# Expert quarters between histogram chunks, and openings that wait only for what they use

## The chip, the cores and the metric

The program runs on one core of a Trainium2 chip. The metric is the device time of one execution in microseconds (us); the times shown are the median and the spread of three runs.

## The reference, cut to what matters

The input is x, 8 images of 32 x 32 tokens with 256 channels (8192 tokens). Four stages follow one another, each with a residual:

```python
x = x + retention(_ln_c(x))            # 8 heads of 32, decayed scores, group norm, gelu, Wo
t = t + moe(_ln_t(t), edges0)          # expert layer 0
x = x + int8_conv_3x3(_ln_c(x))
t = t + moe(_ln_t(t), edges1)          # expert layer 1

def moe(x, ...):
    h = (x @ W_gat).reshape(M, HEADS, NUM_EXPERTS)       # graph attention over 1048576 edges
    e = leaky_relu(a_src[src] + a_dst[dst])
    alpha = exp(e - e_max[dst]) / denom[dst]
    agg = segment_sum(h[src] * alpha, dst) + b_gat
    scores = layernorm(agg).mean over heads              # -> top 2 of 4 experts, softmax
    for ei in range(4):
        hh = gelu(x @ W1[ei] + b1[ei])                   # 256 -> 512
        out += gate[ei] * (hh @ W2[ei] + b2[ei])         # 512 -> 256
```

Edges name nodes up to 65536, and out-of-range indices are clamped for reading and dropped for adding. So an edge counts where its target is one of the 8192 tokens: most of those have the last token as their source and only need to be counted per target (a histogram), and the rest are listed one by one. The experts' products need no edge, so TensorE can do them in any gap before the gates are known.

## The kernel before, in words

The program is written in raw engine queues: each engine (SP, POOL, ACT, DVE, PE) has one instruction stream and waits on semaphores; the order of the work is the order in the source. The functions are `attention_layer`, `ffn_layer` (twice) and `conv_layer`, with a barrier of all engines between them.

**Attention.** `turn(-1)` is the opening: it loads the first image, makes its statistics (DVE `statistics`, `variances`), the power on POOL (L279), the normalised image on ACT (`normal`, L337), its transposes and first projections on PE (L604, L542). The eight images follow in turns 0 to 7. Ahead of `turn(-1)`, DVE centres the value weights (L475 to L480) and waits for the rotation tables (`s_rot_t`), ACT and PE wait for the small constants (`s_small`: `blk`, `sel`, `gb`), which SP loads last of all, behind 7.5 MB of decay tables (L220 to L225).

**Expert layer.** Tokens stand in 16 blocks of 512. 64 pairs (block, expert) are to be computed; the first 40 (`PRE_PAIRS`) are done while the graph part runs, 16 in the window loop, the last 8 with the gates known. A pair is 16 quarters: `fourths(n, ...)` on PE (L1144) issues n quarters, of which two of four are one up-product each (`up`, L1128) and two are two down-products each (`down`, L1139); `experts(n)` and `pre(n)` are 4n quarters. The 40 pairs are 656 quarters. ACT follows with the gelu (`gelu`, L1333), eviction and bias, in the same order of pairs.

The stages of a layer, in order, with what PE gets between its own work (all by `pre`):
1. Opening: SP loads the first block of x, its edges, 15 constants, then block 1 (L933 to L956). DVE, ACT and PE wait for all 15 (`s_const`, L1166, L1376, L1499).
2. Nodes, 16 blocks: DVE moments, edge scan, normalising; PE transposes and `heads`; quarters by `PRE_NODES`.
3. Lists: DVE takes the largest 8 of each segment, three times; 33 x 4 quarters (`PRE_LISTS`).
4. Halves: 52 half-steps that rank and place list entries; PE gets 2 quarters in each.
5. Unit: one more list unit (`unit_products` L1250 on PE, `unit_places` on DVE, four half-steps that pass results back and forth). PE does `pre(PRE_UNIT)` = 24 quarters before it. DVE then sorts (`sort`), makes the targets and releases POOL (`turn_to_next`).
6. Rounds: four times, DVE takes eight keys of each of 32 segments (`eights_of_key`), their digits, and 8 pairs of one-hot matrices (`hots`, L1525); PE multiplies each pair into the histogram (`chunk`, L1199). DVE may be two pairs ahead. PE does `pre(PRE_ROUND)` = 52 quarters before the 8 chunks.
7. Late chunks and the open loop: one more pass of keys, two smaller chunks, then a loop of `n_round` passes, which runs twice here. PE does `pre(PRE_LATE)` = 72 quarters ahead of the late chunks.
8. Window: counts, the last 24 quarters, another unit, then the segmented scans on DVE, for which POOL has gathered rows since stage 5 (64 scatters L1066, 168 gathers L1073). PE runs the 16 looped pairs; ACT stops inside them for two exponentials, the first after `IN_SCAN` = 6 steps (`s_xm`).
9. Gates and tail.

## Time and profile before

| | |
|---|---|
| median of three runs | 4097.9 us (4090.67 to 4099.19) |
| profiled execution, its own time | 4094.64 us |
| its span | 4092.9 us, 49913 instructions |
| PE busy, DVE busy | 86%, 71% of the span |
| mean granted TensorE clock | 0.935 |
| attention / expert layer 0 / conv / expert layer 1 | begin at about 0, 1250, 2546 and 2792 us |

A row of the timeline gives its start in us from the beginning of the span, its length, the engine, the line of the kernel, what is written and read, and how many instructions are merged in it; the bracket is the time the engine stood idle before, and what ended that. A product in float32 appears as two records, so 4 records of L1128 are two up-products, and 8 of L1139 four down-products.

### The profile page before, as it was taken

The page shows a single profiled execution, that of the slowest core. Times are in us where ns is not written, and L with a number is a line of the kernel's source. Part 1 is how long each engine was busy: PE and PEld are TensorE (multiplying, and loading weights), DVE is VectorE, ACT ScalarE, POOL GpSimd, SP SyncE. Part 2 cuts the span into 40 slices and gives each one's busy share as a digit, 9 for nine tenths or more (in the row PEclk, how much of TensorE's full clock was granted, in tenths as well). Part 3 has the DMA queues.
Part 4 walks back from the last instruction along what each step waited for, and adds up shares of the span by engine and source line. Part 5 has one row for each costly group of instructions (what it writes and reads, how often), then busy time and mean ns, then how long its engine had stood idle before and what let it go on. Part 6 is the DMA issues. An engine that isn't in the chain of part 4 may idle for free. (4 is left out here: it accounts for less than half of the span.)

```text
span 4092.9 us, 49913 instructions
## 1 busy us (share of the span) xinstructions
PE 3513.5 (86%) x16818; PEld 2016.4 (49%) x16818; DVE 2885.9 (71%) x6290; ACT 1489.9 (36%) x2073; POOL 1616.9 (40%) x1146
## 2 busy tenths in 40 slices
PE   4999999999985999969878987585999969878987
PEld 2233333333324765646555654464665646555655
DVE  2676676676666798797779336876788797778337
ACT  2565565555552632212223321231632212223321
POOL 2776676666770000058863401000000048872500
PEclk9999999999995999989989998786999989989999
DMA  3000000010005410001121347215410001122337
GB/s 145 11 22 11 32 32 13 20 32 22 11 21 200 163 53 27 32 22 41 32 62 56 138 147 280 78 64 199 174 48 32 32 22 36 37 42 70 138 133 273
DMA packets 151250, 307.24 MB, mean 75 GB/s; under 512 B 24932, under 2 KB 107492, under 8 KB 145892
## 3 DMA queue, kind: packets, MB, share of 16 engines
q1 hardware_dynamic: 100516, 186.28, 12.7%
q10 hardware_dynamic: 25920, 94.38, 6.0%
q0 software_dynamic: 24576, 23.41, 3.3%
q8 instruction: 149, 2.44, 0.3%
q14 instruction: 89, 0.73, 0.1%
HBM read 186.18 MB, written 117.83 MB: 74 GB/s over the span
## 5 line engine op out<-in xcount | busy, mean ns | idle before, releaser
L1128 PE MATMUL l_pu<-l_tt,l_w 128*128 128x512 f32 x2048 | 1005.3, 612 | 52.7 <-ACT l_hid L1333 38.9
L1139 PE MATMUL l_pd<-l_w,l_hid 128*128 128x256 f32 x4096 | 985.2, 383 | 12.2 <-ACT l_hid L1333 12.2
L1139 PEld LDWEIGHTS l_pd<-l_w,l_hid 128*128 128x128 f32 x4096 | 782.2, 193 | 310.9 <-issue 226.7
L1333 ACT ACTIVATE l_hid<-l_pu,l_b 128x512 f32<-128x512 f32 x512 | 349.9, 687 | 1177.7 <-PE l_pu L1128 1170.1
L389 DVE TENSOR_TENSOR at_pr<-at_ps,at_decay 128x1024 f32<-128x1024 f32 x512 | 600.7, 1215 | 179.7 <-PE at_ps L503 178.7
L307 ACT ACTIVATE at_ab<-at_pr 128x1024 f32<-128x1024 f32 x512 | 537.1, 1055 | 435.6 <-DVE at_pr L389 392.1
L258 POOL TENSOR_TENSOR at_ab<-at_ab 128x1024 f32<-128x1024 f32 x256 | 601.2, 2372 | 176.8 <-ACT at_ab L307 176.8
L1128 PEld LDWEIGHTS l_pu<-l_tt,l_w 128*128 128x128 f32 x2048 | 388.4, 196 | 322.7 <-issue 300.4
L1073 POOL DMA_INDIRECT l_g<-hs_rows,l_i_src x336 | 409.6, 1219 | 102.5 <-issue 102.5
L1066 POOL DMA_INDIRECT spots<-l_ad,l_i_row x128 | 160.4, 1253 | 608.2 <-DVEq L1731 569.8
L503 PE MATMUL at_ps<-at_qr,at_kr 32*128 32x512 f32 x2048 | 348.9, 643 | 13.9 <-issue 8.9
L1199 PE MATMUL l_ph<-l_one_lo,l_one_hi 128*128 128x256 bf16 x1104 | 137.3, 281 | 172.1 <-DVE l_one_hi L1525 172.1
L522 PE MATMUL at_ps_av<-at_pr,at_v 128*32 128x512 f32 x2048 | 277.0, 608 | 6.9 <-ACT at_o L315 5.1
L1525 DVE TENSOR_TENSOR l_one_lo<-l_iota,l_lo 128x4096 bf16<-128x4096 bf16 (+1 forms) x72 | 158.1, 2196 | 123.8 <-PE l_ph L1199 123.1
L542 PE MATMUL at_ps<-at_xnT,at_wt 128*128 128x512 f32 x512 | 239.0, 610 | 6.8 <-DVE at_t L410 4.1
L1347 ACT ACTIVATE l_yst<-l_pd 128x512 f32<-128x512 f32 x224 | 133.8, 597 | 249.9 <-PE l_pd L1139 249.9
L503 PEld LDWEIGHTS at_ps<-at_qr,at_kr 32*128 32x128 f32 x2048 | 106.7, 184 | 234.0 <-issue 168.0
L1358 ACT ACTIVATE l_pd<-l_b 128x512 f32<-128x512 f32 x256 | 153.9, 601 | 168.9 <-DVEq L1967 114.6
L1199 PEld LDWEIGHTS l_ph<-l_one_lo,l_one_hi 128*128 128x128 bf16 x1104 | 106.3, 100 | 202.6 <-DVE l_one_hi L1525 187.9
L1954 DVE SCALAR_TENSOR_TENSOR l_xo<-l_yb,l_gates,l_xo 128x256 f32<-128x256 f32 x448 | 187.3, 480 | 15.5 <-DMA l_yb<-ys 7.9
L1082 POOL DMA_INDIRECT l_res<-found,l_i_row x128 | 122.7, 958 | 180.1 <-DMA found<-l_rows 141.7
L542 PEld LDWEIGHTS at_ps<-at_xnT,at_wt 128*128 128x128 f32 x512 | 92.9, 191 | 153.7 <-issue 125.6
(362 smaller groups left out, 4169.2 us busy)
## 6 DMA issues: line engine op xcount, KB each, us to landing
ys<-l_yst ACTq DMA_DIRECT2D x112, 512.0 KB, 2.7
l_yb<-ys SPq DMA_DIRECT2D x28, 2048.0 KB, 10.1
l_tt<-tT ACTq DMA_DIRECT2D x36, 512.0 KB, 3.4
at_xt<-in_x SPq DMA_DIRECT2D x16, 1024.0 KB, 5.3
l_xt<-x SPq DMA_DIRECT2D x32, 512.0 KB, 4.1
tT<-l_xnT ACTq DMA_DIRECT2D x32, 512.0 KB, 4.6
l_xo<-x SPq DMA_DIRECT2D x28, 512.0 KB, 4.9
x<-at_xt SPq DMA_DIRECT2D x8, 1024.0 KB, 4.3
```

What stands on the lines that cost most here:

```text
L258: pool.tensor_tensor(size(2 * k, p), size(2 * k, p), size(2 * k + 1, p), ALU.add).then_inc(s_sum, 1)
L307: act.activation(size(n // 2, n % 2), pr[:, n % 4, :, :], ACT.Abs).then_inc(s_a, 1)
L389: dve.tensor_tensor(pr[:, n % 4, :, :], ps[slot("s", n)][:, :, :], decay[:, h:h + 2, first:first + HALF], ALU.mult).then_inc(s_ring[slot(" ...
L503: ins = pe.matmul(ps[slot("s", n)][:, jj, :], kr[rows, hq, P * kb:P * kb + P], qr[rows, hq, HALF * qn:HALF * qn + HALF], start=True, stop= ...
L522: ins = pe.matmul(ps_av[KD * j:KD * j + KD, :], v[:, kb, KD * h:KD * h + KD], pr[:, (2 * u + j // 2) % 4, j % 2, :], start=(kb == 0), stop ...
L542: ins = pe.matmul(ps[slot(what, i)][:, s, :], wt[:, 2 * (i // 2) + s, k, P * hq:P * hq + P], xnT[:, k, HALF * (i % 2):HALF * (i % 2) + HAL ...
L1073: pool.indirect_dma_start(g[:, j, :], None, hs_rows[:, :], bass.IndirectOffsetOnAxis(ap=i_src[:, j:j + 1].bitcast(U32), axis=0)).then_inc( ...
L1128: ins = pe.matmul(ps_u[q % 2][:, :], w1[:, e, c, P * q:P * q + P], tt[:, s, c, :], start=(c == 0), stop=(c == KK - 1))
L1139: ins = pe.matmul(ps_d[r // 2][:, C * (r % 2):C * (r % 2) + C], hid[:, k % 2, c, P * r:P * r + P], w2[:, k % GE, c, :], start=False, stop= ...
L1199: ins = pe.matmul(hist, one_hi[:, q % 2, j:j + 2, :].rearrange("p a b -> p (a b)"), one_lo[:, q % 2, j:j + 2, :].rearrange("p a b -> p (a ...
L1333: act.activation(hid[:, k % 2, q, :], ps_u[q % 2][:, :], ACT.Gelu, bias=b1[:, k % GE, q:q + 1]).then_inc(s_act, 1)
L1954: ins = dve.scalar_tensor_tensor(xo[:, b, r, :], yb[:, b, MTT * q + r, :], gates[:, MTT * t + r, q:q + 1], xo[:, b, r, :], ALU.mult, ALU.add)
```

## The change

- Attention: the ten small loads go from SP, behind the decay tables, to POOL's queue, ahead of its `turn(-1)`. ACT and PE wait for them after `turn(-1)`. DVE centres the values after the statistics (at u = 18), and PE waits for `s_cen` at the projections.
- Expert layer, opening: `ident` has its own semaphore and is loaded after block 0; block 1 goes ahead of the other constants; `w_gat`, `att_src`, `att_dst` and `iota` are loaded by ACT's queue. DVE does moments and normalising of block 0, then the score columns, then the scan. All other constants are waited for at block 2 (ACT) or after the nodes (DVE, PE).
- Quarters on PE (ACT's order of work is the same, its split into calls is dropped): the stage of lists and halves is unchanged.

| quarters | before | after |
|---|---|---|
| ahead of the unit | 24 | 0 |
| after the unit | 0 | 52 |
| each round, ahead of its chunks | 52 | 32 |
| each round, after each of 8 chunks | 0 | 2 |
| ahead of the late chunks | 72 | 40 |
| ahead of the open loop | 0 | 20 |
| left for the window | 24 | 24 |

```diff
-ROUNDS1 = 0
-PRE_ROUND = 13
+PRE_ROUND = 8
+PRE_CHUNK = 2
-PRE_LATE = 18
-PRE_UNIT = 6
+PRE_LATE = 10
+PRE_OPEN = 5
+PRE_UNIT = 13
...
@@ attention, SP and POOL
-            sp.dma_start(blk[:, :], blk_in).then_inc(s_small, 16)
-            sp.dma_start(sel[:, :], sel_in).then_inc(s_small, 16)
-            for j in range(HPQ):
-                sp.dma_start(gb[KD * j:KD * j + KD, 0:1], ln_g).then_inc(s_small, 16)
-                sp.dma_start(gb[KD * j:KD * j + KD, 1:2], ln_b).then_inc(s_small, 16)
...
             pool.memset(nhalf[:, :], -0.5).then_inc(s_cst, 1)
+            pool.dma_start(blk[:, :], blk_in).then_inc(s_small, 16)
+            pool.dma_start(sel[:, :], sel_in).then_inc(s_small, 16)
+            for j in range(HPQ):
+                pool.dma_start(gb[KD * j:KD * j + KD, 0:1], ln_g).then_inc(s_small, 16)
+                pool.dma_start(gb[KD * j:KD * j + KD, 1:2], ln_b).then_inc(s_small, 16)
@@ attention, ACT and PE
-            act.wait_ge(s_small, 16 * (2 + 2 * HPQ))
             turn(-1)
+            act.wait_ge(s_small, 16 * (2 + 2 * HPQ))
...
-            pe.wait_ge(s_cen, 1)
-            pe.wait_ge(s_small, 16 * (2 + 2 * HPQ))
             turn(-1)
+            pe.wait_ge(s_small, 16 * (2 + 2 * HPQ))
@@ experts, PE
             def histogram(s_at):
                 for q in range(RC // HIST):
                     chunk(q, HIST, s_at(q))
+                    pre_part(PRE_CHUNK)
...
-            pre(PRE_UNIT)
             unit_products(xu, n_u)
+            pre(PRE_UNIT)
-            for r in range(ROUNDS1, ROUNDS0):
+            for r in range(ROUNDS0):
                 pre(PRE_ROUND)
                 histogram(lambda q: r * (RC // HIST) + q + 1)
             pre(PRE_LATE)
             for k, width in enumerate(LATE_CHUNKS):
                 chunk(CHUNKS0 + k, width, CHUNKS0 + k + 1)
+            pre(PRE_OPEN)
             pe.wait_ge(s_round, 1)
@@ experts, DVE
-            dve.wait_ge(s_mem, 1)
-            dve.wait_ge(s_const, CONSTS)
...
-            for b in range(NBLK):
+            moments(0)
+            normal(0)
+            score_columns()
+            scan(0)
+            for b in range(1, NBLK):
                 moments(b)
                 scan(b)
                 normal(b)
-                if b >= 1:
-                    drain(b - 1)
+                drain(b - 1)
             drain(NBLK - 1)
+            dve.wait_ge(s_mem, 1)
+            dve.wait_ge(s_const, CONSTS)
@@ experts, ACT
-            act.wait_ge(s_const, CONSTS)
-            act.wait_ge(s_open, 2)
+            act.dma_start(wg[:, :, 0:GF], w["w_gat"]).then_inc(s_gat_in, 16)
+            act.dma_start(a_s[:, :], w["att_src"].to_broadcast([P, GF])).then_inc(s_gat_in, 16)
+            act.dma_start(a_d[:, :], w["att_dst"].to_broadcast([P, GF])).then_inc(s_gat_in, 16)
+            act.dma_start(iota[:, :], consts["iota_row"]).then_inc(s_gat_in, 16)
```

How the instructions of an engine stand in the program (no times in these rows; the lines of the changed kernel are shifted by 5 to 7 in this part):

PE at the end of the halves and the unit, before (`l_pr` are the banks of ranks and of the table, L1276 reads the count of units):

```order
L1232 MATMUL l_pr<-l_sent,l_one 128x336 x3
L1270 MATMUL l_ph<-l_zero 128x256
L1276 TENSOR_LOAD l_n_unit
L1276 ISA x2
L1128 MATMUL l_pu<-l_tt,l_w 128x512 x2
L1139 MATMUL l_pd<-l_w,l_hid 128x256 x4
```

and of the change:

```order
L1239 MATMUL l_pr<-l_sent,l_one 128x336 x3
L1277 MATMUL l_ph<-l_zero 128x256
L1280 TENSOR_LOAD l_n_unit
L1280 ISA x2
L1259 UNCONDITIONAL_BRANCH
L1259 ISA
L1225 MATMUL l_pr<-l_one,l_above 128x384
L1227 MATMUL l_pr<-l_one,l_ones 128x256
```

The unit's first product now follows the load of the count; the 24 quarters that stood between are gone from here.

PE in a round, before: the 8 chunks of 16 products in one piece, with quarters on both sides (`l_ph` is the histogram bank):

```order
L1128 MATMUL l_pu<-l_tt,l_w 128x512 x2
L1139 MATMUL l_pd<-l_w,l_hid 128x256 x4
L1199 MATMUL l_ph<-l_one_lo,l_one_hi 128x256 x128
L1128 MATMUL l_pu<-l_tt,l_w 128x512 x2
L1139 MATMUL l_pd<-l_w,l_hid 128x256 x4
```

and of the change:

```order
L1144 MATMUL l_pd<-l_w,l_hid 128x256 x4
L1204 MATMUL l_ph<-l_one_lo,l_one_hi 128x256 x16
L1133 MATMUL l_pu<-l_tt,l_w 128x512 x2
L1204 MATMUL l_ph<-l_one_lo,l_one_hi 128x256 x16
L1144 MATMUL l_pd<-l_w,l_hid 128x256 x4
L1204 MATMUL l_ph<-l_one_lo,l_one_hi 128x256 x16
```

Each chunk is now followed by two quarters, in turn two up-products and four down-products.

ACT in the attention's opening, before, with what it waits for:

```order
L337 ACT_TABLE_LOAD [waits at_rstd]
L337 ACTIVATE at_xn<-at_xt,at_shift,at_rstd 128x256 [waits at_small]
```

and of the change:

```order
L337 ACT_TABLE_LOAD
L337 ACTIVATE at_xn<-at_xt,at_shift,at_rstd 128x256 [waits at_rstd]
```

The table load waits for nothing any more, and the small constants are waited for at the first magnitude of turn 0.

## Rows read from the trace of the kernel before

**Rows 1.** The page's part 1: engines' busy time, share, instructions.

```profile
PE 3513.5 (86%) x16818; PEld 2016.4 (49%) x16818; DVE 2885.9 (71%) x6290; ACT 1489.9 (36%) x2073; POOL 1616.9 (40%) x1146
```

**Rows 2.** Timeline of layer 0, PE, expert quarters: start, us, engine, line, out<-in, count.

```profile
1840.79 1.89 PE L1139 MATMUL l_pd<-l_w,l_hid 128*128 128x256 f32 x8
1842.51 1.88 PE L1128 MATMUL l_pu<-l_tt,l_w 128*128 128x512 f32 x4
```

**Rows 3.** Timeline, PE, histogram chunks of layer 0; in brackets idle time before.

```profile
1806.62 6.49 PE L1199 MATMUL l_ph<-l_one_lo,l_one_hi 128*128 128x256 bf16 x32 [29.19 <-DVE l_one_hi L1525]
...
1876.95 3.66 PE L1199 MATMUL l_ph<-l_one_lo,l_one_hi 128*128 128x256 bf16 x32
...
1945.58 3.66 PE L1199 MATMUL l_ph<-l_one_lo,l_one_hi 128*128 128x256 bf16 x32
```

**Rows 4.** Timeline, DVE, the round between: eight largest per segment, then the one-hot pairs.

```profile
1830.29 10.54 DVE L1535 MAX8 l_cand<-l_key 128x8 f32<-128x256 f32 x32
...
1855.38 2.29 DVE L1525 TENSOR_TENSOR l_one_lo<-l_iota,l_lo 128x4096 bf16<-128x4096 bf16 x1
...
1858.73 2.29 DVE L1525 TENSOR_TENSOR l_one_lo<-l_iota,l_lo 128x4096 bf16<-128x4096 bf16 x1
```

**Rows 5.** Timeline, DVE, the unit of layer 0.

```profile
1721.74 0.29 DVE L1640 SCALAR_TENSOR_TENSOR l_sent<-l_pr,l_one 128x128 f32<-128x128 f32 x1 [18.33 <-PE l_pr L1220]
```

**Rows 6.** Timeline, DVE and PE, late chunks and open loop: layer 0, then layer 1.

```profile
2036.92 10.55 DVE L1535 MAX8 l_late<-l_key 128x8 f32<-128x256 f32 x32
...
2067.31 2.29 DVE L1525 TENSOR_TENSOR l_one_lo<-l_iota,l_lo 128x4096 bf16<-128x4096 bf16 x1
...
2102.90 1.23 DVE L1525 TENSOR_TENSOR l_one_lo<-l_iota,l_lo 128x2048 bf16<-128x2048 bf16 x1 [11.21 <-PE l_ph L1199]
...
3668.02 1.89 PE L1199 MATMUL l_ph<-l_one_lo,l_one_hi 128*128 128x256 bf16 x8 [20.12 <-DVE l_one_hi L1525]
...
3671.54 3.73 PE L1128 MATMUL l_pu<-l_tt,l_w 128*128 128x512 f32 x4
```

**Rows 7.** Instructions of one line, POOL's indirect DMAs of layer 0, with times to landing.

```profile
L1066 POOL DMA_INDIRECT spots<-l_ad,l_i_row x64: 955/962/3037, 1778.8 to 1877.4; - x64
...
L1073 POOL DMA_INDIRECT l_g<-hs_rows,l_i_src x168: 942/947/3037, 1878.6 to 2133.4; - x168
...
DMA to landing us min/median/max: 2.3/2.7/4.6
```

**Rows 8.** Timeline, DVE, first use of the gathered rows, layer 0.

```profile
2172.46 1.54 DVE L1823 TENSOR_TENSOR l_e<-l_g,l_adj 128x672 f32<-128x672 f32 x1 [0.55 <-DVE l_adj L1818]
```

**Rows 9.** Timeline, ACT of layer 1, after the gathered rows are used.

```profile
3722.03 1.28 ACT L1414 ACT_TABLE_LOAD   x1 [1.22 <-DVE l_xm L1830]
```

**Rows 10.** Timeline, the attention's opening; then DMAs to landing, POOL's own issues.

```profile
18.30 2.71 DVE L431 BATCH_NORM_STATS2 at_stats<-at_xt 128x6 f32<-128x256 f32 x8 [6.12 <-DMA at_sin<-in_sin]
...
22.24 1.67 POOL L279 TENSOR_TENSOR at_rstd<-at_ve,at_nhalf 128x8 f32<-128x8 f32 x1 [21.34 <-DVE at_ve L443]
...
38.13 4.04 ACT L337 ACTIVATE at_xn<-at_xt,at_shift,at_rstd 128x256 f32<-128x256 f32 x8 [12.57 <-DMA at_gb<-in_ln_b]
...
at_decay<-in_decay SPq DMA_DIRECT2D x2, 3840.0 KB, 27.3
at_xt<-in_x SPq DMA_DIRECT2D x2, 1024.0 KB, 5.4
...
L1045 POOL DMA_DIRECT2D hs_rows<-l_hs x32: 750/752/963, 1282.9 to 2972.6; - x32
```

**Rows 11.** Timeline, DVE and SP, opening of expert layer 0; x to landing.

```profile
1249.99 0.37 SPq L933 DMA_DIRECT2D l_xt<-x  x1
...
1263.88 0.29 DVE L1500 CAST l_pc<-l_iota 128x128 f32<-128x128 bf16 x1 [19.51 <-DMA l_b<-in_L_b]
...
1273.71 1.39 DVE L1455 BATCH_NORM_STATS2 l_stats<-l_xt 128x6 f32<-128x256 f32 x4
...
l_xt<-x SPq DMA_DIRECT2D x10, 512.0 KB, 4.3
```

More of the change, by code:

```diff
@@ L449, in invert, with centre_values @@
                     dve.reciprocal(sd[:, cols], sd[:, cols]).then_inc(s_rsd, 1)
+                def centre_values():
+                    dve.wait_ge(s_wt, 16)
+                    wv = wt[:, 4, :, :].rearrange("p k (h d) -> p (k h) d", d=KD)
+                    dve.tensor_reduce(vsum[:, :], wv, AX.X, ALU.add).then_inc(s_csum, 1)
+                    dve.wait_ge(s_csum, 1)
+                    dve.scalar_tensor_tensor(wv, vsum[:, :].unsqueeze(2).to_broadcast([P, KK * H, KD]), -1.0 / KD, wv,
+                                             ALU.mult, ALU.add).then_inc(s_cen, 1)
+                    dve.wait_ge(s_rot_t, 64)
                 for u in range(NQ):
+                    if b == -1 and u == 18:
+                        centre_values()
                     if tail and u == SPREAD + 1:
@@ L538, in project @@
                 def project(what, hq, i):
+                    if b == -1:
+                        pe.wait_ge(s_cen, 1)
                     pe.wait_ge(s_ring[slot(what, i)], free(what, i))
@@ L940, in _ @@
             block_edges(0)
-            for into, from_ in ((ident, consts["ident"]), (first, consts["first"]), (above, consts["above"]), (not_above, consts["not_above"]), (places, consts["places"]), (iota, consts["iota_row"]),
+            sp.dma_start(ident[:, :], consts["ident"]).then_inc(s_ident, 16)
+            block_x(1)
+            block_edges(1)
+            for into, from_ in ((first, consts["first"]), (above, consts["above"]), (not_above, consts["not_above"]), (places, consts["places"]),
                             (part, consts["part"])):
                 sp.dma_start(into[:, :], from_).then_inc(s_const, 16)
-            sp.dma_start(wg[:, :, 0:GF], w["w_gat"]).then_inc(s_const, 16)
-            sp.dma_start(a_s[:, :], w["att_src"].to_broadcast([P, GF])).then_inc(s_const, 16)
-            sp.dma_start(a_d[:, :], w["att_dst"].to_broadcast([P, GF])).then_inc(s_const, 16)
             for k, v_ in enumerate((w["b_gat"], w["ln_gamma"], w["ln_beta"])):
@@ L1731, in turn_to_next @@
                 dve.sem_inc(s_first, 1)
-            rounds(0, ROUNDS1)
-            restart()
             unit_places(xu, n_u)
```

46 lines of the change are left out of this document (18 added, 28 removed).

## The prediction

> **What bounds the kernel now.** I read the page first. PE is busy for 86% of the span [rows 1], so an average says PE; but the product work is a fixed stock, and what matters is where PE waits and where it makes DVE wait. So I went through the timeline of PE and DVE, stage by stage, then asked on which engine each wait ends.
>
> A unit of four quarters is 1.72 us of down-products and 1.72 us of up-products, one starting at 1840.79 and the next at 1842.51 [rows 2]: a quarter is 0.86 us. 656 quarters of a layer are 564 us of PE.
>
> A round lasts 68.6 us, from 1876.95 to 1945.58 [rows 3]. PE's own work in it is 52 quarters (44.7 us) and 8 chunks. A chunk is 16 products; two back to back take 3.66 us, so one costs about 1.8 us. That is 59 us. DVE's work is 25.1 us of keys and digits (1830.29 to 1855.38) and 8 pairs of one-hots, one every 3.35 us (1855.38 to 1858.73) [rows 4], together 52 us. Neither engine fills the round. DVE may be only two pairs ahead, so it stands still while PE finishes its 52 quarters, and then PE stands still for about 1.5 us in each of six chunks (3.35 less 1.8). In round 0 PE waited 29.19 us for the first pair [rows 3], and after that wait its products ran at the lower level of the clock: 32 of them took 6.49 us instead of 3.66.
>
> Three more places have the same look. In the unit DVE waits 18.33 us for PE [rows 5], which is still in its 24 quarters. At the open loop DVE waits 11.21 us for the late chunks, and then PE 20.12 us for DVE [rows 6]. At the openings everything waits for a load it doesn't use: ACT for `gb` until 38.13 though POOL's result was there at 24.2 [rows 10], DVE for `b2` until 1263.88 though x was asked for at 1249.99 [rows 11].
>
> One chain runs beside all this: POOL's 64 scatters and 168 gathers, from 1778.8 to 2133.4 [rows 7]. DVE uses their result at 2172.46, held then only by its own scan [rows 8]. With 0.95 us for the last issue and 2.7 us to land [rows 7], the rows are there at 2137.0; DVE is ready at 2171.9 (2172.46 less 0.55). POOL's slack is 34.9 us. This number decides the size of the gain.
>
> **The change, part by part** (times of layer 0; layer 1 repeats them within 0.5 us).
>
> *Attention opening.* x lands at 1.2 + 5.4 = 6.6 us [rows 10]. From the start of the statistics to the end of POOL's part is 5.9 us (18.30 to about 24.2). POOL now issues ten loads first. The nearest row is its own plain issue of 0.75 us [rows 10]; with the 0.3 us between its issues, ten end at about 11.4, later than DVE's 10.3. The power (1.67) and the product (0.2) then end at 13.4. ACT's table load waits for nothing now. `normal` starts at about 13.9 instead of 38.13: 24 us earlier. Everything up to the first scores follows from it: projections at 22.4, `s_cen` at about 12 (the weights landed at 10.8), rotation tables at 18.3, decay tables at the latest near 37 (median 27.3 us after issue), while the first weighing would be at 56. Bounds: issues of 0.96 us and 0.5 us between them cost 4 us more; nothing excludes 25 us. I take -24, ends -18 and -25.
>
> *Expert openings.* x lands 4.3 us after its issue in this stage [rows 11], at 1254.4; moments 1.9 us, root 0.3, normalising 1.6, score columns 1.2, scan 4.9: block 1 begins at about 1264.5 instead of 1273.71 [rows 11], 9.2 us earlier. Block 2's x and edges stand behind 4 MB of weights and 1.3 MB of blanks in SP's queue; I take 1.2 us of lateness for them, between none and 5 (the 5.4 us of a 1 MB load). So -8 per layer, ends -4 and -9.3. The stages after it are led by DVE until the halves (the quarters of the lists, 132 of 0.86 us, run out before DVE is done), so the gain is passed on.
>
> *Unit.* 24 quarters (20.7 us) go from ahead of it. DVE's wait of 18.33 us [rows 5] shrinks to a hand-over of about 0.6: -17.7 per layer, ends -16 and -18.3. The quarters go into the gap behind: 84 of them (72.3 us) now stand before the first chunk, which becomes ready 74 us after the unit. PE's wait of 29.19 us is gone; the clock stays up.
>
> *Rounds.* PE has 32 quarters (27.5 us) and 8 times chunk and two quarters (1.76 + 1.72 = 3.48 us, 27.9 us): 55.4 us per round, PE-bound, with DVE's 52 beside it. From the first chunk (28.0 us after POOL's start) round 0 ends 27.9 later, three more at 55.4: 222.1 us after POOL's start, against 259.5 before.
>
> *Late chunks and open loop.* 40 quarters (34.4 us) equal DVE's pass of keys and first pair (from 2036.92 to 2067.31 + 3.4, 33.8 us, with 0.7 us of small work ahead) [rows 6]. The chunks come at 256 us, 20 quarters follow (17.2 us), and DVE's two loop passes of 21 us (PE's wait of 20.12 and a chunk [rows 6]) no longer wait for PE: DVE ends them at 295.6 us after POOL's start; before it was 347.1 (2102.90, the pair's 1.9 and another 21.1). DVE's path alone becomes 51.5 us shorter.
>
> *What is late next.* POOL. Its chain doesn't shrink with the rounds: it starts with `turn_to_next`, ahead of them. A gather takes 947 ns and at most 3037 [rows 7]; the long ones fall on the one-hot pairs, of which POOL gets one issue through each: 232 issues at 1.25 us are 290 us, and some 30 pairs at 2.1 us make up the rest of the 358 us. The pairs come every 3.48 us now, which adds 0.14 to each (4.3 us), and DVE's unit and copies fall into the chain's end (2 us, an estimate between none and the 15 of the second rival). So the rows are ready 364.5 us after its start; DVE was ready for them at 393.3. The gain after POOL's start is 28.8 us, not 51.5. DVE, ACT (which had waited just 1.22 us for `s_xm` [rows 9]) and PE behind it stand still for the difference of 23 us.
>
> The Trainium skill, SBUF — State Buffer, "Terms", has it that VectorE and GpSimd share a port pair under an exclusive lock, held for the whole instruction, and the loser blocks entirely. By the row's median of 947 ns the sum below stands; by that rule each conflicting DVE instruction delays a gather and the total is that of the second rival.
>
> After 20.12 us of waiting PE ran at the lower level: four records took 3.73 us instead of 1.88 [rows 2, 6], and the next eight were slow too, 2.4 us lost. The same befalls PE behind the new wait, now on the path that counts. Net -26.4 per layer after POOL's start; ends -15 and -36.
>
> *Sum.* 24 + 2 x (8 + 17.7 + 26.4) = 128.2 us. Against the profiled execution's own 4094.6 that is 3966.4; this execution lies 3.3 us below the median of three and inside their 8.5 us; it would be 3970 against the median, and I say 3968.
>
> **The rivals.**
> - *POOL's chain is no bound.* Its long issues could vanish if the gaps between pairs suffice. For: they depend on DVE's spacing, which changes. Against: the pairs remain, 32 of them. DVE's full 51.5 and no slow clock: 2 x 25.1 us more, 3918 us.
> - *POOL's chain grows.* DVE's copies, unit and spot products now run while gathers are issued. If 12 DVE instructions hold one back by a long pair's share (1.25 us each), that is 15 us per layer: 3998 us. This is what the Trainium skill's rule on the shared port pair would do here. Against: the median gather is 947 ns though DVE works through nearly the whole chain [rows 7].
> - *Openings give less.* Ten issues on POOL, or tiny loads that queue behind decay tables all the same, hold the first image to 14 us gained; block 2 waits 5 us for its x: 3968 + 10 + 10 = 3988 us.
> - *Slower: quarters between chunks hold up the histogram.* Every up-product waits for ACT's gelu two steps back, and with a chunk between, PE's switch from one kind to the other could cost. 32 such steps per layer; POOL's chain hides the first 23 us. The whole gain of 64 us per layer is gone when a step takes (23 + 64) / 32 = 2.7 us more than 3.48, from 6.2 us on. At 7 us it would be 3968 + 2 x (112.6 - 23) = 4147 us. Against: in the halves PE switches after every quarter already, and ACT needs far less time for a quarter than PE (it is busy for 36% of the span, PE for 86% [rows 1]).
> - *The change doesn't do what it says.* ACT, whose order isn't altered, could be the one that paces PE. Then rounds keep 68.6 us and only openings and unit count: 24 + 2 x 25.7 = 75 us, 4020 us. Against: ACT waits for PE, with 50 points less to do [rows 1].
>
> **How the numbers follow.** Forecast 0.71, POOL grows 0.11, openings give less 0.08, POOL no bound 0.05, doesn't do what it says 0.03, slower 0.02. The forecast's own ends: the attention's spread of 1 to 6, and per layer 1 to 4, 1 to 2 and 10 to 11, taken together as independent, give 3946 to 3990; the second and third rivals carry the upper end to 3998. Below 3945 lies only the first rival, above only the last two: 3945 to 3998. A measurement of this kernel tells from no change what exceeds about 0.2%, 8 us. Every case but one is faster by far more: faster 0.97, slower 0.02, the same 0.01.
>
> **What would show it.** In the profile after: the first `normal` near 14 us; the second block's moments about 9 us closer to the layer's first load; no wait of DVE in the unit over 2 us; rounds of 55 to 56 us with PE idle under 2 us each; POOL's chain from first scatter to last gather 358 to 366 us; DVE waiting some 20 us for a DMA (the gathered rows) at its first use of them, the one new long wait; ACT at `s_xm` likewise. Wrong would be: a round above 60 us (then PE's switching costs), no such wait on DVE (POOL is no bound, more gain), or a chain of POOL above 375 us.

## The result and the profile after

The changed kernel takes 3941.3 us (median of 4 runs, 3939.7 to 3943.6) against 4095.6 us before: ratio 0.962, interval 0.961 to 0.964, 154 us less. The direction was right, and the size was not: 3968 us had been predicted, and the time lies 4 us below the low end of the range. The profiled execution spans 3940.0 us against 4092.9, which is 152.9 us less; the accounts below are made with these two. Experiments 1 to 4 and six more of the runs below were made on chips where DVE and PE are slow for as long as POOL's chain runs, and the kernel before takes 4762 to 4765 us: of them the text uses stretches that lie outside the chain, and the difference to the kernel before on the same chip.

The page's part 1 of the changed kernel: the same instructions in less time. POOL is busy for 25 us less than before (1592 us instead of 1617), PE for 14 us less (its mean granted clock is 0.940 instead of 0.935), DVE and ACT for about as long as before.

```profile
PE 3499.4 (89%) x16818; PEld 2012.8 (51%) x16818; DVE 2891.3 (73%) x6290; ACT 1489.8 (38%) x2073; POOL 1592.2 (40%) x1156
```

The attention's opening, in the timeline (start, us, engine, line, operation; in brackets the idle time before). It answers to [rows 10].

```profile
6.07 0.50 POOL L286 DMA_DIRECT2D at_gb<-in_ln_b  x1
11.16 1.68 POOL L274 TENSOR_TENSOR at_rstd<-at_ve,at_nhalf 128x8 f32<-128x8 f32 x1 [4.60 <-DVE at_ve L443]
...
13.16 4.04 ACT L337 ACTIVATE at_xn<-at_xt,at_shift,at_rstd 128x256 f32<-128x256 f32 x8 [11.13 <-POOL at_shift L276]
```

POOL's ten issues are over at 6.57 us, before DVE has its sums at 11.00, and `normal` starts at 13.16 instead of 38.13. The first load of the expert layer is issued at 1227.27 instead of 1249.99.

The expert opening, layer 0, SP and DVE, for [rows 11]:

```profile
1227.27 0.37 SPq L940 DMA_DIRECT2D l_xt<-x  x1
...
1236.24 0.43 SPq L958 DMA_DIRECT2D l_w<-in_L_w  x1
...
1239.91 0.52 SPq L940 DMA_DIRECT2D l_xt<-x  x1
1241.43 6.88 SPq L944 DMA_DIRECT2D l_src<-in_L_edges  x1
...
1241.49 1.40 DVE L1459 BATCH_NORM_STATS2 l_stats<-l_xt 128x6 f32<-128x256 f32 x4
...
1257.52 1.40 DVE L1459 BATCH_NORM_STATS2 l_stats<-l_xt 128x6 f32<-128x256 f32 x4 [7.21 <-DMA l_xt<-x]
...
1261.13 0.43 DVE L1487 TENSOR_SCALAR l_ib<-l_dst 128x512 int32<-128x512 int32 x1 [1.59 <-DMA l_dst<-in_L_edges]
```

Its DMA view from 1227 to 1260 us (KB each, median us to landing):

```profile
DMA packets 6168, 10.95 MB, mean 332 GB/s; under 512 B 2191, under 2 KB 4233, under 8 KB 5909
...
l_xt<-x SPq DMA_DIRECT2D x4, 512.0 KB, 9.4
```

The second block's moments start 14.2 us after the layer's first load instead of 23.7, as predicted. But the third block's start at 30.3 and wait 7.21 us for x and 1.59 for edges: its loads were issued at 1239.91 and 1241.43, behind both weights (1236.24 is the first), and the issue of `src` alone took SP 6.88 us. The median of the four loads of x is 9.4 us to landing here, not 4.3. By the last block DVE is 0.5 us earlier than before (159.1 instead of 159.6 us after the first load), by the lists 0.4 us (273.5 and 273.9), in layer 1 0.9. "The lists" stands here and below for DVE's first maximum over the picked entries (`l_m<-l_picked`), close to the end of stage 3.

The unit and the rounds, DVE and PE, for [rows 3 to 5]:

```profile
1677.69 0.17 DVE L1625 TENSOR_SCALAR l_bits<-l_lu 128x12 int32<-128x12 int32 x1 [1.48 <-DVEq L1690]
...
1765.19 1.92 PE L1204 MATMUL l_ph<-l_one_lo,l_one_hi 128*128 128x256 bf16 x16 [1.67 <-DVE l_one_hi L1535]
...
1820.51 1.91 PE L1204 MATMUL l_ph<-l_one_lo,l_one_hi 128*128 128x256 bf16 x16
...
1875.83 1.91 PE L1204 MATMUL l_ph<-l_one_lo,l_one_hi 128*128 128x256 bf16 x16
...
1822.46 2.29 DVE L1535 TENSOR_TENSOR l_one_lo<-l_iota,l_lo 128x4096 bf16<-128x4096 bf16 x1 [2.19 <-PE l_ph L1204]
1824.67 1.22 DVE L1535 TENSOR_TENSOR l_one_hi<-l_iota,l_hi 128x2048 bf16<-128x2048 bf16 x1
1825.93 2.29 DVE L1535 TENSOR_TENSOR l_one_lo<-l_iota,l_lo 128x4096 bf16<-128x4096 bf16 x1
```

In the unit no wait of DVE is longer than 1.48 us (18.33 before). PE waits 1.67 us for the first pair instead of 29.19, and its first products run at the upper level of the clock (granted 1.00 from 1765 to 1773 us; 0.60 from 1806 to 1814 before). A round lasts 55.3 us (1820.51 to 1875.83), and DVE waits 2.19 us for PE in it.

POOL's chain and the first use of `g`, for [rows 7, 8]; minimum, median and maximum of an issue in ns, then first and last start:

```profile
L1071 POOL DMA_INDIRECT spots<-l_ad,l_i_row x64: 957/962/3037, 1737.4 to 1843.2; - x64
...
L1078 POOL DMA_INDIRECT l_g<-hs_rows,l_i_src x168: 941/947/3028, 1844.5 to 2076.8; - x168
```

The timeline, DVE, and the DMA view from 2050 to 2078 us:

```profile
2085.59 1.54 DVE L1831 TENSOR_TENSOR l_e<-l_g,l_adj 128x672 f32<-128x672 f32 x1 [4.96 <-DMA l_g<-hs_rows,l_i_src]
```

```profile
l_g<-hs_rows,l_i_src POOLq DMA_INDIRECT x22, 9.4
```

This is where the prediction fell. The chain lasts 340.4 us (1737.4 to 2077.8); it was 355.5 before, and had been predicted to grow. The rows of the last gathers take 9.4 us to land where they took 2.7, and DVE waits 4.96 us for them, where 23 had been predicted. In layer 1 that wait is 0.80 us, hardly more than DVE's own hand-over of 0.55: there DVE's path and POOL's end together. From the chain's start to the first use of `g` it is 348.2 us, 45.5 less than before. What the prediction had not looked at is SP, which issues its four loads of spots (1.3 MB) at 2044.79 now, while the last gathers run; before it did so at 2137.90, behind the last one. The slow landings begin with these loads; no run separates the two.

| stretch | before | after | difference | predicted |
|---|---|---|---|---|
| to the first load of layer 0 | 1249.99 | 1227.27 | -22.7 | -24 |
| first load to lists, both layers | 548.0 | 546.6 | -1.4 | -16 |
| lists to POOL's first scatter, both | 509.6 | 472.4 | -37.2 | -35.4 |
| POOL's first scatter to first use of `g`, both | 787.4 | 696.1 | -91.3 | -52.8 |
| the rest | 997.9 | 997.6 | -0.3 | 0 |

### The profile page after: what moved, and what is told of

The parts are those of the page before. It is cut to its first block and busy times, and to the rows that moved or that the text cites. A ratio compares the mean times of both kernels' runs of the same rounds, so it can differ in the third digit from the quotient of the medians.

```text
span 3940.0 us, 49916 instructions
## 1 busy us (share of the span) xinstructions
PE 3499.4 (89%) x16818; PEld 2012.8 (51%) x16818; DVE 2891.3 (73%) x6290; ACT 1489.8 (38%) x2073; POOL 1592.2 (40%) x1156
## 5 line engine op out<-in xcount | busy, mean ns | idle before, releaser
L1071 POOL DMA_INDIRECT spots<-l_ad,l_i_row x128 | 175.4, 1370 | 571.1 <-DVEq L1741 532.7
L1078 POOL DMA_INDIRECT l_g<-hs_rows,l_i_src x336 | 364.7, 1085 | 102.4 <-issue 102.4
L507 PE MATMUL at_ps<-at_qr,at_kr 32*128 32x512 f32 x2048 | 349.3, 645 | 13.9 <-issue 8.9
L538 PE MATMUL at_ps_dn<-at_ab,at_roots 128*32 128x512 f32 x1024 | 140.5, 622 | 23.3 <-POOL at_ab L253 23.2
```

Of the source, the lines that this page charges most:

```text
L507: ins = pe.matmul(ps[slot("s", n)][:, jj, :], kr[rows, hq, P * kb:P * kb + P], qr[rows, hq, HALF * qn:HALF * qn + HALF], start=True, stop= ...
L1071: pool.indirect_dma_start(spots[k][:, :], bass.IndirectOffsetOnAxis(ap=i_row[:, 0, 1, c:c + 1].bitcast(U32), axis=0), ad[:, c, :], None).t ...
L1078: pool.indirect_dma_start(g[:, j, :], None, hs_rows[:, :], bass.IndirectOffsetOnAxis(ap=i_src[:, j:j + 1].bitcast(U32), axis=0)).then_inc( ...
```

## The experiments

The theory after this reading. **Gap theory:** POOL gets a second issue into the time of one of DVE's pairs only where DVE leaves a gap between two pairs. In the kernel before, pairs follow each other without one. In the changed kernel PE sets their pace from round 1 on, each pair starts 0.04 us after the one before it has ended, and POOL gets two issues per pair instead of one. Its rival: the chain is shorter because rounds are. **Queue theory**, for the openings: the loads of blocks 2 and 3 stand behind 4 MB of weights and 1.3 MB of blanks. Its rival: the bytes take their time in whatever order they come.

The changed kernel alone holds both cases of the first theory. Round 0, where DVE sets the pace, and round 1, POOL and DVE:

```profile
1765.13 3.03 POOL L1071 DMA_INDIRECT spots<-l_ad,l_i_row  x1 [0.30 <-issue]
1768.47 3.03 POOL L1071 DMA_INDIRECT spots<-l_ad,l_i_row  x1 [0.30 <-issue]
...
1767.26 1.21 DVE L1535 TENSOR_TENSOR l_one_hi<-l_iota,l_hi 128x2048 bf16<-128x2048 bf16 x1
1768.39 2.28 DVE L1535 TENSOR_TENSOR l_one_lo<-l_iota,l_lo 128x4096 bf16<-128x4096 bf16 x1
...
1825.89 0.96 POOL L1071 DMA_INDIRECT spots<-l_ad,l_i_row  x1 [0.30 <-issue]
1827.16 1.89 POOL L1071 DMA_INDIRECT spots<-l_ad,l_i_row  x1 [0.30 <-issue]
...
1828.14 1.22 DVE L1535 TENSOR_TENSOR l_one_hi<-l_iota,l_hi 128x2048 bf16<-128x2048 bf16 x1
```

`one_hi` of 1767.26 ends at 1768.47, after `one_lo` of 1768.39 has begun: no gap, one issue of 3.03 us per pair. In round 1 `one_hi` ends at 1825.89 and `one_lo` starts at 1825.93: an issue of 0.96 us starts in just that instant, and one of 1.89 follows it. The rows say more than the theory does. An issue that starts while `one_lo` runs ends 0.90 us after the next `one_hi` has started: the first of them 1768.16 against 1767.26, the last 1829.05 against 1828.14. This holds for all 70 such issues of the changed kernel's two chains, which last 1.46 to 3.04 us and end 0.90 to 0.92 us behind that start, and for the 70 of the kernel before (0.89 to 0.92). The next issue is ready 0.30 us later, 1.21 us behind the start of `one_hi`. Without a gap the next `one_lo` has begun 0.08 us before that, and holds the issue for nearly its whole length. With the gap the issue starts 0.04 us ahead of `one_lo` and takes 0.96 us. So nearly every pair holds one issue in either kernel (there are 72 pairs), and the gap lets one more in ahead of it. Of the issues of 3 us there are 10 in the changed kernel's chain and 24 in the one before.

**1. The attention part alone.** The kernel before with the hunks of `attention_layer`.

> The kernel before with the attention part of the change alone. If the attention term stands by itself, the first expert load starts 22.7 us earlier (1227.3 instead of 1250.0 us) and the whole kernel is 22 to 23 us shorter, with both expert layers as long as before. If part of it only came together with the other parts, less: under 18 us.

Measured 4740.4 us beside 4764.8, ratio 0.994 (0.993 to 0.996): 24.4 us less. The first expert load is issued at 1226.97 us, and the lists start 273.4 us later (before: 273.9). The part stands by itself, and its size was right.

**2. The openings alone.** The kernel before with the new order of loads and of DVE's first block.

> The kernel before with the expert openings alone. Queue theory: block 1 starts 9.5 us earlier after the layer's first load, but block 2's tokens stand behind 4 MB of weights and 1.3 MB of blanks, so that the maxima over the lists start only 0.4 us (layer 0) and 0.9 us (layer 1) earlier and the whole kernel gains 1 to 2 us. The prediction's theory (lateness of 1.2 us): 8 us per layer, 16 us in all.

Measured 4763.7 us beside 4764.8, ratio 1.000 (0.999 to 1.001). Blocks 1 and 2 begin 14.8 and 32.9 us after the first load in layer 0, the lists at 275.9, which is 2 us later than before; in layer 1 at 273.1, which is 1 us earlier. The change's openings are worth nothing that can be measured.

**3. The weights later.** The changed kernel; `found` and the blanks go behind block 6 in the same way.

```diff
-            sp.dma_start(w1[:, :, :, :], w["w1"]).then_inc(s_w, 16)
-            sp.dma_start(w2[:, :, :, :], w["w2"]).then_inc(s_w, 16)
             for b in range(2, NBLK):
...
                 block_edges(b)
+                if b == 2:
+                    sp.dma_start(w1[:, :, :, :], w["w1"]).then_inc(s_w, 16)
+                if b == 3:
+                    sp.dma_start(w2[:, :, :, :], w["w2"]).then_inc(s_w, 16)
```

> The changed kernel, with the two 2 MB weight loads behind the loads of blocks 2 and 3 and the blanks behind block 6. Queue order theory: block 2's moments start about 21 us after the layer's first load instead of 30.2, and the 8 us last to the lists: 8 us per layer, 14 to 17 us less in all. Bandwidth theory (10 MB have to pass before the nodes can run freely, whatever the order): a later block waits as long, and the gain is under 4 us in all.

Block 2 starts 23.2 us after the first load instead of 30.3, block 3 at 32.2 instead of 40.9, the last at 149.5 instead of 159.1, the lists at 263.9 and 264.1 instead of 273.5 and 273.2. That is 9.6 and 9.1 us per layer: the queue theory holds, and no later block gives it back. The whole time is 4608.9 us beside 4761.6; what the edit is worth on a chip without the slowness, experiment 7 shows.

**4. The unit alone.**

```diff
-            pre(PRE_UNIT)
             unit_products(xu, n_u)
+            pre(PRE_UNIT)
```

> The kernel before with one edit: the 24 quarters ahead of the unit stand behind it. DVE's wait of 18.3 us in the unit goes, PE's wait for the first pair of one-hots shrinks from 29.2 us to about 9, and POOL's chain starts 18 us earlier with the same 355 us length: 36 us less in all. If the unit's gain needs the rest of the new placing, because rounds come too early and DVE just waits there for PE, it is under 20 us.

From the lists to the first scatter it is 237.2 us instead of 254.9, 17.7 less, which is all that the whole change gains there (18.3). Of the whole time the ratio is 0.995 (0.994 to 0.997), 22 us, since on this chip the stretch behind is slow. So the step is confirmed, and the whole's 36 us is not.

**Four more runs on these chips.** Their question lies under POOL's chain, where the chips are slow. The placing alone:

> The kernel before with the new places of PE's quarters alone. If the terms add up, what attention (22.7) and openings (1.3) don't explain of 152.9 us comes from here: 129 us less, with POOL's chain 340 us long. By the prediction's terms (17.7 + 26.4 per layer, POOL's chain 364 us) it would be 88 us.

Measured 4653.8 us beside 4764.8. DVE's gap (the edit of experiment 6) in the changed kernel:

> The changed kernel, where DVE also waits for its own last pair of one-hots before the next one in a round. Gap theory (POOL gets two issues per pair instead of one when DVE's pairs don't follow without a gap): the seven or eight issues of 3.03 us in round 0 become 1.9 us as in rounds 1 to 3, POOL's chain goes from 340 to about 331 us, the wait of 5 us at the first use of g in layer 0 goes, DVE's path is 1 us longer: 2 to 5 us less in all. Theory that POOL's chain shrank because PE paces the rounds, not because of the gap: round 0 keeps its 3.03 us issues, chain 340 us, time the same or 2 us more.

Measured 4624.8 us beside 4761.6. One quarter behind a chunk:

> The changed kernel with one quarter behind each chunk instead of two, and 40 ahead of the round instead of 32. DVE paces the chunks again. Gap theory: POOL's issues of 3.03 us come back in rounds 1 to 3, the chain is 352 to 358 us long, rows come 15 us later, rounds last about 59 us, and the kernel is 25 to 32 us slower than the changed one. If the number of quarters ahead of DVE has nothing to do with POOL: chain 340 to 344, DVE's own rounds set the time, 18 to 24 us slower.

Measured 4654.4 us beside 4761.6. The gap in the kernel before:

> The kernel before, where DVE waits for its own last pair of one-hots before the next in a round; nothing else. Gap theory: the 26 issues of 3.03 us fall to under 5, and POOL's chain goes from 355.6 to 340 us or less though rounds stay at 68.6 to 69.5 us; the chain has 35 us of slack, so the time doesn't gain: the same, or up to 8 us slower by the longer pairs (0.12 us x 7 x 4 per layer). If the shorter rounds were what shortened the chain, it stays at 354 to 358 us.

Measured 4765.4 us beside 4761.6. None of them tells the theories apart: the chain lasts 297 to 302 us in all, whatever the pairs do. The first, third and fourth come again below; the second is part of kernel 7.

**5. The changed kernel again.**

> The changed kernel once more, in a job with the kernel before, since the eight runs so far stand beside a kernel before of 4762 to 4765 us instead of 4096: while POOL's chain of gathers runs, DVE there starts an instruction every 0.7 or 1.4 us and PE one product every 2.8 us, which the traces of 4092.9 and 3940.0 us don't show. If this belongs to the chips of those two jobs, this run gives 3941 us beside 4096. If it is here too, the changed kernel gives about 4626 us beside 4762 (the openings and the attention part gain as before, the placing under POOL's chain gains less).

Measured 3940.5 us beside 4098.2, ratio 0.961 (0.960 to 0.963). The slowness belongs to those chips; all runs from here on, but two in experiment 10, stand beside a kernel before of 4095 to 4099 us.

**6. A gap without shorter rounds.** The kernel before; DVE waits until its own last pair is done.

```diff
                         if r * EACH + q >= 2:
                             dve.wait_ge(s_hist, r * EACH + q - 1)
+                        if q >= 1:
+                            dve.wait_ge(s_one, r * EACH + q)
                         hots(q, HIST * q, HIST)
```

> The kernel before with DVE's wait for its own last pair, again, in a job in which DVE and PE aren't slow under POOL's chain (before at 4098 us). Gap theory: the 26 issues of 3.03 us fall to under 5, most of them to 1.9 us, and POOL's chain goes from 355.6 to 340 us or less though rounds stay at 68.6 to 69.5 us; the chain has 35 us of slack, so the time is the same or up to 8 us longer. If it was the shorter rounds that shortened the chain: 354 to 358 us.

The timeline of a round in it, DVE and POOL:

```profile
1888.93 1.22 DVE L1525 TENSOR_TENSOR l_one_hi<-l_iota,l_hi 128x2048 bf16<-128x2048 bf16 x1
1890.25 2.29 DVE L1525 TENSOR_TENSOR l_one_lo<-l_iota,l_lo 128x4096 bf16<-128x4096 bf16 x1
...
1890.13 0.94 POOL L1073 DMA_INDIRECT l_g<-hs_rows,l_i_src  x1 [0.30 <-issue]
1891.38 1.98 POOL L1073 DMA_INDIRECT l_g<-hs_rows,l_i_src  x1 [0.30 <-issue]
```

The instructions of POOL's two lines in it:

```profile
L1066 POOL DMA_INDIRECT spots<-l_ad,l_i_row x64: 955/962/2694, 1785.7 to 1876.5; - x64
...
L1073 POOL DMA_INDIRECT l_g<-hs_rows,l_i_src x168: 941/947/2876, 1877.8 to 2112.5; - x168
```

`one_hi` ends at 1890.15 and the next `one_lo` starts at 1890.25. Not one issue of 3.0 us is left, and the chain lasts 327.7 us instead of 355.5, in rounds of 69.6 us. The rival (354 to 358) has fallen. DVE pays 0.19 us per pair for it (one every 3.53 us instead of 3.34), 1 us per round. The time is 4099.7 us beside 4096.4, ratio 1.001 (1.000 to 1.002): 28 us of a chain that nobody waits for are worth nothing, as expected.

**And shorter rounds with the gap closed.** The changed kernel with `PRE_ROUND = 10` and `PRE_CHUNK = 1`.

> The changed kernel with one quarter behind each chunk and 40 ahead of a round, again, beside before at 4098 us. Gap theory: the 3.03 us issues come back in rounds 1 to 3, the chain is 352 to 358 us long, DVE waits for the gathered rows, rounds last about 59 us: 3966 to 3973 us. If the pairs' spacing has nothing to do with POOL: chain 338 to 344 us, DVE's own rounds set the time: 3958 to 3964 us.

The timeline of round 1, PE and POOL, and the first use of `g`:

```profile
1833.69 1.91 PE L1204 MATMUL l_ph<-l_one_lo,l_one_hi 128*128 128x256 bf16 x16
...
1842.45 1.92 PE L1204 MATMUL l_ph<-l_one_lo,l_one_hi 128*128 128x256 bf16 x16 [0.55 <-DVE l_one_hi L1535]
...
1892.86 1.91 PE L1204 MATMUL l_ph<-l_one_lo,l_one_hi 128*128 128x256 bf16 x16
...
1839.07 3.03 POOL L1071 DMA_INDIRECT spots<-l_ad,l_i_row  x1 [0.30 <-issue]
...
2107.80 1.54 DVE L1831 TENSOR_TENSOR l_e<-l_g,l_adj 128x672 f32<-128x672 f32 x1 [6.56 <-DMA l_g<-hs_rows,l_i_src]
```

POOL's line of gathers in it:

```profile
L1078 POOL DMA_INDIRECT l_g<-hs_rows,l_i_src x168: 940/944/3062, 1852.4 to 2099.9; - x168
```

PE waits 0.55 us for each pair, so DVE sets the pace, and the issues of 3.03 us are back (26 in this chain, 10 in the changed kernel's). The chain lasts 360.3 us (357.7 in layer 1), 20 and 17 more than in the changed kernel; rounds 59.2 us (1833.69 to 1892.86); DVE waits 6.56 us for the rows. The time is 3977.6 us, ratio 0.970 (0.969 to 0.972), a little above the 3966 to 3973 of the gap theory; in layer 0 the chain came out 2 us longer than the 352 to 358 I had for it, and in layer 1 within them.

**7. Both remedies.** Weights later and DVE's gap, on the changed kernel.

> The changed kernel with both later edits: weights behind blocks 2 and 3, blanks behind block 6, and a wait of DVE for its own last pair of one-hots. On a chip that runs the changed kernel in 3941 us: 3920 to 3925 (16 from the weights, 2 to 5 from the gap). Where DVE and PE are slow under POOL's chain: 16 us less than the changed kernel, nothing from the gap.

The timeline, DVE: the third block's moments, with no wait ahead of them, and the first use of `g`; then POOL's two lines.

```profile
1256.05 1.41 DVE L1462 BATCH_NORM_STATS2 l_stats<-l_xt 128x6 f32<-128x256 f32 x4
...
2081.69 1.54 DVE L1836 TENSOR_TENSOR l_e<-l_g,l_adj 128x672 f32<-128x672 f32 x1 [0.55 <-DVE l_adj L1831]
```

```profile
L1074 POOL DMA_INDIRECT spots<-l_ad,l_i_row x64: 954/958/2930, 1733.5 to 1827.1; - x64
...
L1081 POOL DMA_INDIRECT l_g<-hs_rows,l_i_src x168: 940/944/2897, 1829.4 to 2063.7; - x168
```

Measured 3920.9 us beside 3940.5 for the changed kernel on the same chip; ratios to before 0.957 (0.955 to 0.958) and 0.961 (0.960 to 0.963). The chain lasts 331.3 us and DVE no longer waits for rows (0.55 us, its own hand-over), yet the first use of `g` comes 348.2 and 347.9 us behind the chain's start, as in the changed kernel (348.8 and 348.3 on this chip). 17.3 of the 19.6 us are the weights' (7.7 and 9.6 us between first load and lists), and of the gap's 2 to 5 us there is about 1. Something else holds DVE; experiments 9 and 10 find it.

**8. The placing alone,** again.

> The kernel before with the new places of PE's quarters alone, beside before at 4096 to 4098 us. If the three parts add up, it lacks the 22.7 us of the attention and the 1.3 us of the openings: 129 us less than before, 3967 to 3971 us, POOL's chain 340 us and the first use of g 348 us behind the chain's start. By the prediction's terms (17.7 + 26.4 per layer) 88 us less, 4009 us.

Measured 3967.9 us beside 4094.8, ratio 0.969 (0.967 to 0.970): 126.9 us less. With the attention's 24.4 and the openings' 1.2 the parts make 152.5 of the 154.3 us. The first use of `g` is 350.6 and 345.1 us behind the chain's start. So the parts add up, and the surplus over the predicted 88 us is all in this one.

**9. What bounds it now.** Kernel 7 with two quarters less ahead of each round and eight more in the stage of the lists, behind which PE waits 8.06 us for DVE (8.14 in the changed kernel).

```diff
-PRE_LISTS = 33
+PRE_LISTS = 35
...
-                pre(PRE_ROUND)
+                pre_part(4 * PRE_ROUND - 2)
```

> The kernel with later weights and DVE's wait (3921 us), and 8 quarters more ahead of the lists, where PE waits 8.1 us for DVE, in exchange for two quarters less ahead of each round. If PE paces the rounds (DVE waits 2.2 us for it in each): rounds 1 to 3 take 53.6 instead of 55.3 us, first use of g 5 us earlier per layer, 3909 to 3913 us. If DVE or POOL's chain already sets the time (331 us, then 8 us to land, against DVE ready at 348): 3918 to 3922 us.

The timeline, PE's first chunks of rounds 1 and 2, and DVE behind the open loop:

```profile
1809.11 1.91 PE L1207 MATMUL l_ph<-l_one_lo,l_one_hi 128*128 128x256 bf16 x16
...
1862.70 1.91 PE L1207 MATMUL l_ph<-l_one_lo,l_one_hi 128*128 128x256 bf16 x16
...
2047.58 0.17 DVE L1628 TENSOR_SCALAR l_bits<-l_lu 128x12 int32<-128x12 int32 x1 [17.97 <-DMA l_lu<-more]
```

Rounds take 53.6 us (1809.11 to 1862.70): PE had set their pace. But the first use of `g` comes 347.8 and 345.1 us after the chain's start, only 0.4 and 2.7 us earlier. Instead another wait stands on DVE's path: behind the open loop it waits for the unit's list (6 KB), in layers 0 and 1 for 9.99 and 10.35 us in the kernel before, 11.62 and 15.39 in the changed one, 15.74 and 15.22 in kernel 7, 17.97 and 14.75 here. Where it grew by 2.2 us the first use came 0.4 us earlier, and where it fell by 0.5 us, 2.7. Measured 3907.5 us beside 4094.8, ratio 0.954 (0.952 to 0.955). A second time, beside experiment 10:

> The partner of list_first_2: 3904 to 3911 us as in moved_early if nothing of its gain was chance, 3911 to 3915 us if part was.

3913.1 us beside 4099.1, ratio 0.954 (0.952 to 0.955). By the medians the gain over kernel 7 is 13.5 us the first time and 7.8 the second; by the ratios it is 0.27% and 0.29%, some 11 us, both times. Which part of it was chance the runs don't settle; the stretches of the first profile give about 8.

**10. The list first.** SP has four loads of spots (1.3 MB) ahead of that list; now it has them behind it.

```diff
                 sp.wait_ge(s_next, m + 1)
...
+                n_more = sp.value_load(n_next[0:1, 0:1], min_val=1, max_val=MAXUNIT)
+                unit_loads(xb, n_more, 0)
                 for k in range(SPOTS):
...
-                n_more = sp.value_load(n_next[0:1, 0:1], min_val=1, max_val=MAXUNIT)
-                unit_loads(xb, n_more, 0)
```

> The unit's list loaded ahead of the spots, again, hoping for a chip where the kernel before takes 4095 to 4098 us (the first time it took 4765). If the four loads ahead of it delay the list: DVE's wait for it falls from 15 to 18 us to 5 to 8, first use of g at 339 to 342 us behind the chain's start instead of 347.8 and 345.1, 8 to 15 us less than moved_early. If POOL's gathers hold it in whatever place: 0 to 4 us less.

Kernel 9 in its second profile: DVE's wait in the timeline, then the load in the DMA view of that stretch.

```profile
2053.93 0.17 DVE L1628 TENSOR_SCALAR l_bits<-l_lu 128x12 int32<-128x12 int32 x1 [16.03 <-DMA l_lu<-more]
```

```profile
l_lu<-more SPq DMA_DIRECT2D x1, 6.0 KB, 11.7
```

This kernel: the timeline of SP and DVE, the wait for rows with it, then the same DMA row.

```profile
2032.15 0.36 SPq L1002 DMA_DIRECT2D l_lu<-more  x1
2032.87 3.07 SPq L1016 DMA_DIRECT2D l_pay<-spots  x4
...
2037.32 0.19 DVE L1628 TENSOR_SCALAR l_bits<-l_lu 128x12 int32<-128x12 int32 x1 [6.47 <-DMA l_lu<-more]
...
2069.58 1.54 DVE L1836 TENSOR_TENSOR l_e<-l_g,l_adj 128x672 f32<-128x672 f32 x1 [7.75 <-DMA l_g<-hs_rows,l_i_src]
```

```profile
l_lu<-more SPq DMA_DIRECT2D x1, 6.0 KB, 4.8
```

The wait falls from 16.0 to 6.5 us (13.0 to 6.8 in layer 1), and the first use of `g` comes 342.3 and 338.1 us behind the chain's start instead of 346.1 and 343.3, where it now waits 7.75 us for rows (1.79 in layer 1). 3906.9 us beside 3913.1, ratios to before 0.953 (0.951 to 0.955) and 0.954 (0.952 to 0.955): 6.2 us by the medians, 9 by the two stretches, where 8 to 15 had been expected. The order of SP's loads was the cause of the wait, and POOL's rows are the bound again, in layer 0 above all. By the ratios the two can't be told apart with certainty; this is the fastest kernel of the study, 34 us under the changed one. Both kernels were also measured on a slow chip:

> The fastest kernel so far, where SP loads the unit's list (6 KB) ahead of the four loads of spots (1.3 MB) instead of behind them. The traces show DVE waiting for that list behind the open loop: 10.0 us before the change, 11.6 and 15.4 after it, 18.0 and 14.8 in the fastest kernel, since the load now flies beside gathers and takes 11 to 14 us to land. If the four loads ahead of it are the cause: DVE's wait falls to 5 to 8 us, the rows (chain of 330 us and 8 us to land) set the time again, first use of g at 339 to 342 us behind the chain's start instead of 347.8 and 345.1, 8 to 15 us less in all, 3893 to 3900 us. If it is POOL's gathers that hold the list's load, in whatever place: 0 to 4 us less.

> The same kernel as moved_early, as the partner of list_first in one job: 3904 to 3911 us as the first time. If its 13.5 us below the kernel with both remedies were in part chance, as the expert layers' 7 us in the profiles suggest, 3911 to 3915 us.

4584.4 and 4592.7 us beside 4764.9, ratios 0.963 (0.961 to 0.964) and 0.964 (0.963 to 0.966). POOL's chain is over there some 290 us before DVE waits for the list, so no gather flies beside it. Still DVE's wait falls from 9.99 to 3.60 us (10.16 to 5.44 in layer 1), and the first use of `g` comes 4.4 and 3.0 us earlier. So the loads ahead of the list delay it without any gather, and the second theory, that the gathers hold it in whatever place, has fallen here too.

## Why the prediction missed

- **Attention opening:** -24 predicted, -22.7 in the profile, -24.4 by itself. Right in size, with `normal` at 13.16 us for 13.9, and with some luck: POOL's ten issues were to end at 11.4 us and to be what the power waits for. They ended at 6.57, and it waits for DVE, which was at 11.00 instead of 10.3.
- **Expert openings:** -8 per layer predicted with ends of -4 and -9.3; -0.4 and -0.9 measured. This step failed. The sum for block 1 was right to 0.3 us. What failed is "I take 1.2 us of lateness" for block 2: it was 8.8 us (7.21 and 1.59). I had bounded the lateness of a load behind 4 MB by the 5.4 us of a 1 MB load; the row to take was the sum of bytes in front. In the first 33 us of the layer 10.95 MB pass, at 332 GB/s on the mean; block 2's x, issued at 1239.91, is there at 1257.5, and 7 us earlier when the weights stand behind it (experiment 3). The third rival had 5 us per layer for it, still too small.
- **Unit:** -17.7 per layer predicted, -18.3 and -19.0 measured, -17.7 by itself. Right.
- **Rounds:** 55.4 us predicted, 55.3 measured, no wait of PE in them. Right, and with it the answer to the slower rival: PE's switching between chunks and quarters costs nothing (two quarters and a chunk 3.47 us).
- **DVE's path:** 51.5 us shorter predicted, 49.9 measured (2085.59 less 4.96 less 1737.41 is 343.2; before it was 393.1), and 46.1 in layer 1. What is missing is the growth of its wait for the unit's list (1.6 and 5.0 us), which the prediction did not have.
- **POOL's chain:** the failed step that made the miss. "POOL gets one issue through each [pair] ... The pairs come every 3.48 us now, which adds 0.14 to each" took the issue of 3 us as a property of the pair. It is one of pairs without a gap. The rows were to be ready 364.5 us after the chain's start; they were used at 348.2 and 347.9. The gain behind the chain's start is 45.5 and 45.8 us, where 26.4 net stood. The term for the slow clock (2.4 us) was wrong as well: behind its wait for ACT PE takes 3.75 us for four records at 2099.36, but so it did before at 2186.21, and the rest of the layer is as long as it was. The first rival (POOL no bound, 3918) had the cause in its words, "if the gaps between pairs suffice", at a chance of 0.05, and the prediction's own sign for it, no such wait on DVE, all but came true. The time lies between it and the forecast because the rows landed in 8 us instead of 2.7, because DVE's wait for the unit's list grew, and because the openings gave nothing.
- The sum: 128.2 predicted; attention -1.3, openings -14.6, unit +1.8, chain +38.5, rest +0.3 make the 152.9 us of the profile. Two errors of opposite sign: had the openings given their 16 us, the miss would have been some 40 us instead of 27, and that it is so small is luck.

The Trainium skill, SBUF — State Buffer, "Terms", has the shared port pair locked for a full instruction, and the loser blocked. The traces agree: an issue that starts at 1765.13, 0.07 us behind the start of a `one_lo`, takes 3.03 us, 2.07 more than one that starts 0.04 us ahead of a `one_lo` (0.96). That is about what was left of the instruction, 2.2 us, and it is held by this one alone: it ends within `one_hi`, 0.90 us behind its start. They show when POOL is held, not that it is at the port. The second rival had made of the rule that more DVE work blocks more. The number of issues held stayed as it was (70 in both layers together, before and after); how much of `one_lo` each had still before it changed, and with it the room for a further issue ahead.

## What to carry to other kernels

Where one engine blocks another, look in the trace at when the loser's next instruction is ready and when the winner's next one starts. Here POOL was ready 0.08 us too late, each time; a wait that costs DVE 0.19 us per pair lets POOL start first and gives it a second instruction, and whoever changes who paces the winner changes the loser too. A load that was moved behind a large one is late by the bytes in front of it, not by its own landing time; bulk loads that are needed later belong behind the next small ones. And a gain in a chain that nobody waits for (28 us in experiment 6) is worth nothing until the other path has become shorter: after each step look for the wait that grew.

## What was not expected of the hardware

- A DVE wait for its own last instruction leaves 0.10 us between two pairs and shortens POOL's chain by 28 us of 355. The order of two starts within 0.1 us decides whether an issue takes 0.96 or 3.03 us.
- On three of the seven chips that the experiments ran on, DVE and PE slowed down while the chain ran, and only then. The kernel before takes 4762 to 4765 us on each of the three. The timeline of experiment 3's run, DVE, and of experiment 4's, PE:

```profile
1761.71 0.09 DVE L1552 MATCH_VALUE_LOAD l_key<-l_cand,l_key 128x8 f32 x1 [0.98 <-issue]
1763.11 0.42 DVE L1552 MATCH_REPLACE8 l_key<-l_cand,l_key 128x256 f32<-128x256 f32 x1 [1.31 <-issue]
```

```profile
1861.24 0.27 PE L1199 MATMUL l_ph<-l_one_lo,l_one_hi 128*128 128x256 bf16 x1 [2.53 <-issue]
```

DVE starts an instruction every 1.4 us, PE a product every 2.8 us (2.53 of idle time and 0.27), both with an idle time that ends in nothing the profile shows ("issue"), in experiment 3's run from 15 us after the first scatter to some 18 us after the last gather. POOL's chain takes 297 to 302 us there. On the other four chips neither the kernel before (4095 to 4099 us) nor the changed ones show it. Why stays open.
- A 6 KB load took 11.7 us to land behind 1.3 MB of loads, and 4.8 ahead of them. The gathers land in 9.4 us (median) from 2050 us on, behind SP's loads of those 1.3 MB, and still in 9.9 from 2060 to 2078, where only 8 GB/s pass. Beside a store of ACT's alone (1963 to 1978 us, 71 GB/s) they land in 2.4. Why the delay outlasts the loads stays open.
